# Gated experts sorted into 72 expert tiles through HBM, and a new order of work in the linear attention

## The reference, cut to what matters

```python
qh = split(_layernorm(q @ wq, g, b)); kh = split(_layernorm(k @ wk, g, b)); vh = split(_layernorm(v @ wv, g, b))
q_prime = relu(qh) + EPS_K
k_prime = (relu(kh) + EPS_K) * em
kv = einsum('bhnd,bhne->bhde', k_prime, vh * em)
z = 1.0 / (einsum('bhnd,bhd->bhn', q_prime, k_prime.sum(axis=-2)) + EPS_K)
att = einsum('bhnd,bhde,bhn->bhne', q_prime, kv, z)     # 16 heads of 8
return _layernorm(att.reshape(bsz, -1, 128) @ dense_w + dense_b, g, b)
```

```python
dist = sqrt(max(|xs|^2 + |centroid|^2 - 2 xs @ centroid.T, 1e-12))     # 4096 tokens x 8
w, sel = top_k(dist, 2); w = softmax(w)
we = zeros((T, 8)).at[arange(T)[:, None], sel].add(w)
for e in range(8):
    h = silu(xs @ Wg[e] + bg[e]) * (xs @ W1[e] + b1[e])
    out = out + we[:, e:e + 1] * (h @ W2[e] + b2[e])
```

## Time and profile before

| | us |
|---|---|
| median of 3 runs | 2414.39 (2412.11 to 2418.73) |
| the profiled execution | 2416.86 |
| its span | 2415.0 |
| linear attention, from its first DMA to the next phase's | 213.4 of it |
| gated experts, the same | 591.3 of it |
| mean granted TensorE clock | 0.931 of full |

### The profile page before, as it was taken

The page is one execution under the profiler, slowest core; times in us unless marked ns, Lnnn a source line. Parts: engine busy times, 40 slices in busy tenths (PEclk is TensorE's granted clock), DMA queues, the critical chain, the costliest instruction groups (busy, mean ns, idle before and its releaser), DMA issues.

```text
span 2415.0 us, 49189 instructions
## 1 busy us (share of the span) xinstructions
PE 2139.2 (89%) x19888; PEld 1427.5 (59%) x19888; DVE 1187.9 (49%) x3069; ACT 947.9 (39%) x2431; POOL 546.1 (23%) x510
## 2 busy tenths in 40 slices
PE   3999974875699999799968999999997999999988
PEld 1555564664577788355545555555554666666673
DVE  4566565663412121566544444444443555555558
ACT  1333312563344443233323232333322655655536
POOL 4122114663111110222310101101100223333325
PEclk8999976886699999899989999999998999999979
DMA  4000001000000000200000000000001000000001
GB/s 142 11 11 7 3 1 30 14 1 5 0 2 2 2 1 1 89 12 11 3 2 1 1 0 0 0 0 0 1 1 45 6 5 6 10 5 1 2 1 36
DMA packets 21015, 28.37 MB, mean 12 GB/s; under 512 B 4302, under 2 KB 15574, under 8 KB 20310
## 3 DMA queue, kind: packets, MB, share of 16 engines
q1 hardware_dynamic: 20808, 25.40, 3.4%
HBM read 23.30 MB, written 2.10 MB: 11 GB/s over the span
## 4 chain that ended last, share of the span: by engine, by line
PE 62%; issue 9%; DVE 6%; POOL 3%; POOLq 3%; DVEq 1%; ACT 1%; DMA 1%; SPq 0%; ACTq 0%
PE single L1729 6%; PE quad L1740 5%; PE quad L1741 5%; PE single L1465 4%; PE quad L1453 4%; PE pair L362 3%; PE single L413 2%; PE pair L2054 1%; PE quad L390 1%; PE pair L1412 1%; PE quad L2054 1%; PE single L2066 1%; PE quad L2031 1%; PE quad L2080 1%; PE single L2038 1%
## 5 line engine op out<-in xcount | busy, mean ns | idle before, releaser
L1785 ACT ACTIVATE arena<-quad,arena 114x512 f32<-114x512 f32 x192 | 131.2, 687 | 350.2 <-PE quad L1741 350.1
L1870 DVE SCALAR_TENSOR_TENSOR arena<-quad,arena 114x512 f32<-114x512 f32 x192 | 143.0, 750 | 219.1 <-ACT arena L1785 218.2
L531 DVE TENSOR_REDUCE arena<-pair 128x8 f32<-128x1024 f32 x128 | 156.8, 1225 | 159.4 <-PE pair L362 157.0
L1740 PE MATMUL quad<-arena,wide 128*114 128x512 f32 x384 | 204.3, 613 | 20.4 <-DVE arena L1870 20.4
L238 POOL TENSOR_TENSOR rstd<-var_eps,neg_half 128x4 f32<-128x4 f32 (+1 forms) x64 | 66.0, 1031 | 639.9 <-DVE var_eps L234 544.6
L2287 POOL TENSOR_TENSOR arena<-arena 128x512 f32<-128x512 f32 x128 | 130.5, 1041 | 312.6 <-DVE arena L2210 312.6
L1741 PE MATMUL quad<-arena,wide 128*114 128x512 f32 x384 | 196.9, 594 | 0.0
L1729 PEld LDWEIGHTS single<-wide,arena 114*128 114x128 f32 x1536 | 180.4, 192 | 27.5 <-issue 27.5
L1729 PE MATMUL single<-wide,arena 114*128 114x128 f32 x1536 | 180.6, 275 | 0.0
L613 POOL TENSOR_SCALAR arena<-arena 128x512 f32<-128x512 f32 x56 | 86.8, 1567 | 334.8 <-ACT arena L467 334.8
L513 ACT ACTIVATE arena<-quad 128x1024 f32<-128x1024 f32 x128 | 124.1, 1021 | 70.8 <-PE quad L396 70.7
(11 more groups left out here) (426 smaller groups left out, 4216.9 us busy)
## 6 DMA issues: line engine op xcount, KB each, us to landing
arena<-in_ctxT SPq DMA_DIRECT2D x32, 256.0 KB, 2.7
wide<-in_w SPq DMA_DIRECT2D x2, 2048.0 KB, 10.4
wide<-in_wgu SPq DMA_DIRECT2D x1, 2736.0 KB
x<-in_x SPq DMA_DIRECT2D x4, 512.0 KB, 6.1
out_x<-x SPq DMA_DIRECT2D x8, 256.0 KB, 2.3
wide<-in_w SPq DMA_DIRECT2D x1, 1368.0 KB
we<-in_we SPq DMA_DIRECT2D x1, 512.0 KB, 12.2
wide<-in_wq SPq DMA_DIRECT2D x1, 512.0 KB, 3.7
```

Source lines behind the costliest of these rows:

```text
L531: dve.tensor_reduce(mx[m % 2][:, 8 * p:8 * p + 8], S[:].rearrange("p (h k) -> p h k", h=8), AX.X, ALU.max).then_inc(s["s_free"], 1)
L1740: pe.matmul(bank[2 + k % 2][0:FR, :], wg[:, e, cols], xnT[u], start=True, stop=True)
L1785: act.activation(sg[0:FR, k % 2, :], bank[2 + k % 2][0:FR, :], ACT.Silu, bias=bgc[0:FR, e, f:f + 1]).then_inc(s["sg_ready"], 1)
L1870: dve.scalar_tensor_tensor(out=hid[e % 2][0:FR, f, :], in0=bank[4 + k % 2][0:FR, :], scalar=b1c[0:FR, e, f:f + 1], in1=sg[0:FR, k % 2, :], ...
```

## The change

The gated experts are written anew. All 32 sequences are normalised at once, and the distances, the best two experts and the place of each token among all tokens of its expert are worked out for all 4096 tokens in one go (counts by two matmuls with a triangle and a matrix of ones, then sums on DVE). Each expert gets whole tiles of 128 rows; with 8192 rows for eight experts 2 x 32 + 8 = 72 tiles are always enough. POOL writes each token's row twice to its places in an HBM tensor (64 indirect transfers of 128 rows). A loop over the 72 tiles loads a tile, transposes it, reads the tile's expert into a register, and uses that register for the address of the weights. The biases come as three bfloat16 rows by one extra matmul. Each result tile is stored to a second HBM tensor, and 64 indirect transfers bring the rows back, which DVE adds with their weights. Tiles that no expert needs are computed too.

In the linear attention the same operations stand in another order. PE lifts the first piece of i-1 before `project(i+1)`, projects keys and values before queries, and puts `output(i-2)` one iteration later. ACT's `normed_y(i-2)` moves from the start of its iteration to the end, and the residual follows one iteration later. Some semaphores are shared between two phases, and `clear_twins` clears that set once more in layer 2's attention.

```diff
@@ stages / tensor of linear_attention @@
-                    if 0 <= i + 1 < NG:
-                        project(i + 1)
                     if 0 <= i < NG:
                         turn_q(i)
                     if 0 <= i - 1 < NG:
                         lift(i - 1, 0)
-                        lift(i - 1, 1)
+                    if 0 <= i + 1 < NG:
+                        project(i + 1)
+                    if 0 <= i + 2 < NG:
+                        turn(i + 2)
+                    if 0 <= i - 1 < NG:
+                        for j in (1, 2, 3):
+                            lift(i - 1, j)
                     if 0 <= i < NG:
                         keys_values(i)
-                    if 0 <= i - 1 < NG:
-                        lift(i - 1, 2)
-                        lift(i - 1, 3)
+                    if 0 <= i - 2 < NG:
+                        output(i - 2)
                     if 0 <= i < NG:
                         attend(i)
                     if 0 <= i - 1 < NG:
                         regroup(i - 1)
-                    if 0 <= i + 2 < NG:
-                        turn(i + 2)
-                    if 0 <= i - 1 < NG:
-                        output(i - 1)
@@ gpsimd of linear_attention @@
-                for i in range(-2, NG + 2):
+                for i in range(-2, NG + 3):
+                    if 0 <= i + 1 < NG:
+                        scales(i + 1)
+                        affine_k(i + 1)
                     if 0 <= i - 2 < NG:
                         scales_y(i - 2)
+                    if 0 <= i + 1 < NG:
+                        affine_v(i + 1)
+                    if 0 <= i - 2 < NG:
                         affine_y(i - 2)
...
@@ gated_experts, sync @@
+                for n in range(min(SLOTS, TILES)):
+                    sp.dma_start(xg[n], by_tile[n * P:(n + 1) * P]).then_inc(s[f"landed{n}"], 16)
+                for n in range(TILES):
+                    sp.wait_ge(s["y_copied"], n + 1)
+                    sp.dma_start(done[n * P:(n + 1) * P], ysb[n % SLOTS]).then_inc(s[f"stored{n % SLOTS}"], 16)
+                    if n + SLOTS < TILES:
+                        sp.wait_ge(s["turned"], n + 1)
+                        sp.dma_start(xg[n % SLOTS], by_tile[(n + SLOTS) * P:(n + SLOTS + 1) * P]
+                                     ).then_inc(s[f"landed{n % SLOTS}"], 16)
@@ gated_experts, tensor @@
+                def turn_tile(n):
+                    pe.wait_ge(s[f"landed{n % SLOTS}"], 16 * (n // SLOTS + 1))
+                    if n >= 1:
+                        pe.wait_ge(s["xgT_ready"], n)
+                    pe.transpose(bank[0][:, 0:P], xg[n % SLOTS], ident[:]).then_inc(s["turned"], 1)
+
+                def first(n, e):
+                    pe.wait_ge(s["xgT_ready"], n + 1)
+                    if n >= 2:
+                        pe.wait_ge(s["sg_ready"], n - 1)
+                        pe.wait_ge(s["hid_ready"], n - 1)
+                    for i in range(2):
+                        dst = bank[1 + 2 * i + n % 2][:, 0:F]
+                        pe.matmul(dst, pick[0:65, :], rows[0:65, ds(e * ROW + i * F, F)], start=True, stop=False)
+                        mm = pe.matmul(dst, xgT[n % 2], wide[:, ds(e * STEP + i * F, F)], start=False, stop=True)
+                        mm.then_inc(s["gu_ready"], 1)
...
+                for n in range(-2, TILES + 1):
+                    if 0 <= n + 2 < TILES:
+                        turn_tile(n + 2)
+                    if 0 <= n + 1 < TILES:
+                        expert[n + 1] = pe.value_load(texp[0:1, n + 1:n + 2], min_val=0, max_val=E - 1)
+                        first(n + 1, expert[n + 1])
+                    if 0 <= n < TILES:
+                        turn_hidden(n)
+                    if 0 <= n - 1 < TILES:
+                        second(n - 1, expert.pop(n - 1))
@@ gated_experts, scalar @@
+                def copy_y(n):
+                    act.wait_ge(s["y_ready"], n + 1)
+                    if n >= SLOTS:
+                        act.wait_ge(s[f"stored{n % SLOTS}"], 16 * (n // SLOTS))
+                    act.activation(ysb[n % SLOTS], bank[7][:, 0:P], ACT.Copy).then_inc(s["y_copied"], 1)
@@ gated_experts, gpsimd @@
+                pool.wait_ge(s["slots_ready"], 1)
+                pool.wait_ge(s["zeroed"], 1 + 16 * 8)
+                for n in range(B):
+                    for i in range(2):
+                        pool.indirect_dma_start(by_tile, bass.IndirectOffsetOnAxis(ap=where_i[:, i, n:n + 1], axis=0),
+                                                xn[:, n, :], None).then_inc(s["scattered"], 16)
...
+                for n in range(SLOTS):
+                    pool.wait_ge(s[f"stored{n}"], 16 * (TILES // SLOTS))
+                for g in range(NG):
+                    for n in range(g * G, g * G + G):
+                        for i in range(2):
+                            pool.indirect_dma_start(yg[:, i, n, :], None, done,
+                                                    bass.IndirectOffsetOnAxis(ap=where_i[:, i, n:n + 1], axis=0)
+                                                    ).then_inc(gathered[g], 16)
```

More of the change, by code:

```diff
@@ L1090, in tensor @@
                 pe.wait_ge(s["masks_ready"], 1)
-                for i in range(-2, NG + 1):
+                for i in range(-2, NG + 2):
+                    if 0 <= i < NG:
+                        turn_q(i)
+                    if 0 <= i - 1 < NG:
+                        lift(i - 1, 0)
                     if 0 <= i + 1 < NG:
@@ L1679, in gated_experts @@
[L1679 to L1686 removed]
+            ones, later = arena.take([P]), arena.take([P])
@@ new lines, in gated_experts @@
+            half = arena.take([2 * B])
+            d2, z2, key, sel1, sel2, sel, pos = (arena.take([B, E]) for _ in range(7))
+            scan = [arena.take([B, E]) for _ in range(2)]
+            best, v2z = arena.take([B]), arena.take([B])
+            dist = arena.take([2, B])
+            gap, w1st, w2nd = arena.take([B]), arena.take([B]), arena.take([B])
+            order = arena.take([E])
+            fill, part = arena.take([E, B]), [arena.take([E]) for _ in range(3)]
+            base = arena.take([E])
@@ new lines, in gated_experts @@
+            steps, stepsf = arena.take([P]).bitcast(I32), arena.take([P])
+            where = arena.take([2, B])
+            where_i = arena.take([2, B]).bitcast(I32)
+            texp, texpf = arena.take([TILES]).bitcast(I32), arena.take([TILES])
+            tcmp = arena.take([TILES, E])
+            bias, rest = arena.take([BW]), arena.take([BW])
+            pieces = [arena.take([BW], BF16) for _ in range(3)]
+            rows = arena.take([E * ROW], BF16)
+            pick = arena.take([P], BF16)
@@ L1794, in scalar @@
-                loop(act, group)
+                act.activation(c2, bank[4][:, 0:E], ACT.Copy)
+                for g in range(NG):
+                    act.wait_ge(s["tr_ready"], g + 1)
+                    act.activation(xnT[g % 2], bank[g % 2], ACT.Copy).then_inc(s["xnT_ready"], 1)
+                    for j in range(G):
+                        n = g * G + j
+                        act.activation(sq, xn[:, n, :], ACT.Square, accum_out=sq_sum[:, n:n + 1])
+                        act.drain()
@@ new lines, in vector @@
+                whole = bias[0:BP, :]
+                dve.tensor_copy(pieces[0][0:BP, :], whole)
+                dve.drain()
+                dve.tensor_tensor(rest[0:BP, :], whole, pieces[0][0:BP, :], ALU.subtract)
+                dve.drain()
+                dve.tensor_copy(pieces[1][0:BP, :], rest[0:BP, :])
+                dve.drain()
+                dve.tensor_tensor(rest[0:BP, :], rest[0:BP, :], pieces[1][0:BP, :], ALU.subtract)
+                dve.drain()
+                dve.tensor_copy(pieces[2][0:BP, :], rest[0:BP, :])
@@ L1899, in gpsimd @@
-                root(0)
-                def group(g, u, last):
-                    if not last:
-                        root(g + 1)
-                    pool.wait_ge(s["stats_ready"], g + 1)
-                    rstd_of(pool, g * G)
-                loop(pool, group)
+                pool.memset(rows, 0.0)
+                pool.memset(pick, 0.0)
+                pool.drain()
+                for i in range(3):
+                    pool.memset(pick[32 * i:32 * i + 1, :], 1.0)
+                    pool.drain()
```

538 lines of the change are left out of this document (289 added, 249 removed).

## The result

The changed kernel takes 2638.4 us against 2415.9 us, medians: a ratio of 1.091, 95% interval 1.089 to 1.094. So it is 9% slower, on the side that was held likeliest and inside the range, but 101 us above the forecast. The profiled executions have spans of 2628.2 us and 2415.0 us.

The account below looks back on a forecast made before the run. PE's own work was taken to bound the gated experts, a dependency chain the linear attention. Experts +152, linear attention -30, clears +1 give +123 us on 2416.9, so 2540; less 2.5 to the median, 2537 us, range 2350 to 2770.

Parts of the forecast that it names:

- tile loop and last store: Gated experts: 68 of 75 iterations at a 7.4 us full circle through the load, 523 us in all, plus 2 us.
- gather: Gated experts, after the last store: POOL issues 64 more indirect transfers at 1.25 us each, 80 us.
- last group: End of gated experts: landing 1.9 us, eight additions at 0.28 us, then 2.9 us; with hand-overs 8 us.
- linear attention: Reordered phase: y's chain leaves ACT's path, period 17 us for 22.95 us; -30 us, ends 0 and -50.
- clears of semaphores: Extra clears on POOL at a barrier, +1 us.
- The read: Tile loop: PE's register read stands between transpose and products; 0.8 us a tile, between 0.1 and 1.9 us.
- the clock's term: Tile loop: a mean granted clock of 0.75 turns PE's 2.6 us a tile into 3.45 us.
- The rival with 1.2 GHz throughout: Tile loop and POOL: T = 9.2 us, transfers 2.4 us each, 2806 us; dear transfers and slow clock together 0.15.
- The cheap form of the rival: Scatter and gather: transfers at 0.45 us, with period 6.3 us, 2360 us; 0.25 together with real prefetch.
- the dear one: Scatter and gather: each transfer costs 5.43 us, 3075 us; dear transfers and slow clock together 0.15.
- what is late next: Linear attention: circle of projection, moments, scales, 12 normalisations, turn of q, first lift, next projection; about 14.5 us.
- The rival of a true prefetch: Tile loop: loads off the path, period 4.4 us, 2333 us; "I give it little", 0.25 together with cheap transfers.

## Why the prediction was right in sign and 101 us short

| term | forecast, us | after, us |
|---|---|---|
| front | 48 | 51.0 (1233.1 to 1284.05) |
| scatter and its landing | 82 | 84.0 (to 1368.1) |
| tile loop and last store | 525 | 593.9 (to 1962.0) |
| gather | 80 | 86.4 (to 2048.4) |
| last group | 8 | 12.0 (to 2060.4) |
| sum | 743 | 827.3 |
| less the old phase | +152 | +236.0 |
| linear attention | -30 | -18.9 |
| clears of semaphores | +1 | +3.1 |

These give +220 us; the unchanged phases and the end came out 7 us shorter in this execution, and the difference of the spans is 213 us. The profiled execution was the shortest of four, 8 us below their median.

**The tile loop** holds 69 of the 84 us that the sum of the phase is short. The mechanism was right: one load per tile that is issued behind y, and a full circle from tile to tile. The run with the loads ahead proves it, as it takes 395 us off and keeps all work. The read was near too, 0.8 us forecast and 0.59 us measured as a delay. The Trainium skill, "DMA: Bandwidth & Descriptors", Latency and other measured facts, gives about 600 ns as the floor of such a load; the delay of this case agrees with it, while the read's own row is 0.30 us.

What failed is the clock's term. From the fifth tile on the period is 8.45 us against 7.4, and 68 times the difference are 71 us, the whole of the loop's 69. PE's stretch with the read was to be 3.45 + 0.8 = 4.25 us and has a mean of 5.85 us, 1.6 us more; ACT, SP and the load were to be 3.05 us and are 2.60 us. That is 1.15 us more, less 0.1 us for a slip of the sum: 6.45 us at full clock and 0.85 us for the slower one are 7.3 us, and 7.4 was carried on.

I took 0.75 as a mean clock and divided PE's 2.6 us by it, 3.45 us. The measured mean of the loop, 0.62, would not have been right either, with 4.2 us: it is taken over time, and it counts in the pauses, in every second of which the clock is 1.00. PE's work has to be divided by the clock during the work, 0.54: 4.8 us, and 5.4 us with the read's 0.59. The rest of the miss is PE's own part, counted some 0.5 us too short: with the pause filled and the clock at 0.99 the stretch takes 3.72 us and not 2.6 + 0.59. About 0.1 us of that is the hand-over to ACT, which the sum had among its 3.05 us.

The earlier trace rows had both levels, and the front of the old phase stood at 0.50 throughout in the earlier trace rows; I chose between them by averaging. The rival with 1.2 GHz throughout had T = 9.2 us, near 5.2 + 0.8 + 3.05; its clock was nearer the truth than mine. The lower end, 6.3 us for full clock and a short read, does not follow from its terms either, which are 5.65 + 0.1 = 5.75 us. The filled pause shows the cause: the same chain through the load, PE never idle for long, clock 0.99, and the period falls from 8.16 to 6.17 us.

**The transfers** were priced at 1.25 us from two bounds, 0.44 and 2.47 us, and measured 1.26 us. The bounds were wide; the point between them was as much luck as reading. The cheap form of the rival (0.45 us) and the dear one (5.43 us) are both out; 1.26 us of issue leave no room for them. The estimate of 5.4 us from the Trainium skill, "GPSIMD Engine Reference", Performance pitfalls for Q7 kernels, does not fit these transfers; the measurement decides. The gather's 6.4 us above the forecast are POOL's scales of seven groups between its transfers, about 1 us of power each, which the prediction had left out of the 80 us.

**The last group** ended 4 us later than forecast. The scales of the last group are done at 2055.06, and the next phase begins at 2060.38. POOL's drain at the barrier is the longest of the nine here (min, median, max in ns), where no drain of POOL took over 1105 ns before:

```profile
L117 POOLq DRAIN  x9: 41/1092/6340, 19.0 to 2624.0; - x9
```

It stands behind the phase with the indirect transfers. The three kernels with the old experts have none above 1.11 us, and all five that have 128 indirect transfers have one of 6.34 us. With half the scatters, 96 transfers, it was 8.95 us, so it is not a price per transfer. What causes it was not tried.

**The clears of semaphores** were put at 1 us. POOL's wait at the barrier ahead of the phase is 4.89 us, where it was 1.81 us before and 1.80 us in the run with the linear attention alone, which has only the old clears.

**The linear attention** was forecast at a period of 17 us and -30 us, and gave 19.7 us and -18.9 us. ACT's wait for y went as told. The step that failed is "what is late next": the list had the first lift in its circle but not what that lift waits for while the projection stands queued behind it. The forecast's working has a slip too: 22.95 - 17 is 5.95 us a period, not 5.5. With the projection first the period is 17.5 us and the phase 29 to 32 us shorter than before, which is the forecast's number for another order of work than the change has.

**The rival of a true prefetch** was given little chance, rightly, for this code. As a kernel of its own it is the better one. It was priced at 2333 us and measured 2243.6 us: with the load off the path the clock term goes as well, and so does the read.

## What to carry to other kernels

A ring of buffers prefetches only if its loads are issued ahead of waits on results: look at what the issuing queue waits for, not at the number of slots. A short burst of PE work behind a wait in each iteration costs twice, by the wait and by the low clock in the burst. So price it by the clock that it has during the burst (here 0.54) and not by the mean of the stretch (here 0.62). And a step put first in an in-order queue holds back all that is behind it, even where its own consumer gains.

## What was not expected of the hardware

- An indirect transfer of 128 rows of 512 bytes costs POOL 0.96 us and 0.30 us to the next, 1.26 us, the same at the start and the end of a row of 64 but for its first one (1.26 us and 0.29 us), and for scatter and gather (0.94 to 0.96 us).
- The read of a number into PE's register delays the next matmul by 0.59 us when PE has waited for a load, and by nothing that shows when earlier matmuls are still running (0.11 us from transpose to product with the loads ahead). The read's own row is 0.30 us in both.
- PE work with no use, 12 matmuls a tile, made the kernel 143 us faster by holding the clock at 0.99.
- POOL's drain took 6.3 us at one barrier, against at most 1.1 us before, and 9.0 us with fewer transfers ahead of it.
- The mean clock of a loop says little about one burst: in every second tile here the pause is at 1.00 and in the others at 0.50, while the work is near 0.50 in both.
